# A conditioned residual block on one Trainium2 core: the convolution moved from full-array products on phase-split x to row-tiled, staggered products that read x at a step of 8 bytes

## What is computed

```python
# layer 0: grouped convolution (4 groups of 32 channels, 9 taps, padding 4), residual
out = conv1d(x, weight, padding=4, groups=4)
x   = x + out + (c @ c_weight.T)[:, :, None] + bias[None, :, None]
# layer 1: a 128x128 matrix per sample, mixed from 8 by attention on the condition, residual
att   = softmax(mlp(c))                        # 64 x 8
agg_w = einsum('bk,koi->boi', att, weight)     # one 128x128 matrix per sample
x     = x + einsum('boi,bih->boh', agg_w, x) + (att @ bias_k)[:, :, None]
```

## Time and profile before

| what | value |
|---|---|
| median of 3 runs | 840.06 us (839.46 to 840.33) |
| time of the profiled execution | 839.29 us |
| its span, first to last instruction | 837.4 us |
| TensorE busy (products) | 766.2 us, 92% |
| ScalarE, VectorE, GpSimd busy | 76%, 49%, 66% |
| mean granted TensorE clock | 0.977 of full |
| data moved by DMA | 242.90 MB, 290 GB/s |

### The profile page before, as it was taken

One profiled execution on the slowest core, in us unless ns is written; L12 is line 12 of the kernel. 1 busy time (PEld: TensorE's weight loads), 2 busy tenths in 40 slices (PEclk: granted clock), 3 DMA queues, 4 the chain that ended last, 5 costly groups with the idle time before them and its releaser, 6 DMA issues.

```text
span 837.4 us, 15303 instructions
## 1 busy us (share of the span) xinstructions
PE 766.2 (92%) x5424; PEld 600.9 (72%) x5424; DVE 410.1 (49%) x299; ACT 637.2 (76%) x291; POOL 552.1 (66%) x596
## 2 busy tenths in 40 slices
PE   2659998999999999999999999999999999999994
PEld 2547776777777777777777777777777777777773
DVE  6662455445445555444555445445554444554430
ACT  7766886888778877878786787888777868866554
POOL 3289686667778767767876666668667566866620
PEclk9988999999999999999999999999999999999997
DMA  5778999999999999999999999999999999987643
GB/s 194 206 230 263 309 317 292 305 326 306 325 314 330 313 313 308 318 301 306 329 318 306 297 312 312 319 331 332 305 314 300 284 305 327 319 257 247 220 164 126
DMA packets 91011, 242.90 MB, mean 290 GB/s; under 512 B 15914, under 2 KB 58482, under 8 KB 74610
## 3 DMA queue, kind: packets, MB, share of 16 engines
q1 hardware_dynamic: 90994, 242.67, 91.5%
HBM read 101.57 MB, written 75.50 MB: 211 GB/s over the span
## 4 chain that ended last, share of the span: by engine, by line
SPq 46%; PE 20%; DMA 20%; ACT 6%; issue 6%; POOL 1%; DVE 0%; POOLq 0%
SPq L240 34%; DMA mix_dram<-mix_parts 16%; PE ps L366 12%; SPq L264 9%; PE ps L383 8%; DMA mix_rep<-mix_dram 3%; ACT z_out L448 3%; SPq L272 2%; ACT x_ph L429 1%; ACT x_cv L452 1%; DMA x_in<-in_x_dram 1%; ACT z_out L452 0%; SPq L214 0%; PE ps L353 0%; POOL mix_prod L646 0%
## 5 line engine op out<-in xcount | busy, mean ns | idle before, releaser
L448 ACT ACTIVATE z_out<-ps,par 128x2048 f32<-128x2048 f32 x64 | 253.3, 3957 | 143.0 <-PE ps L383 143.0
L515 DVE TENSOR_TENSOR y_lo<-ps,y_hi 128x1024 fp32r<-128x1024 f32 x128 | 156.4, 1222 | 305.9 <-ACT y_hi L438 305.9
L429 ACT ACTIVATE x_ph<-x_in 128x2048 f32<-128x2048 f32 x63 | 246.5, 3914 | 0.0
L366 PE MATMUL ps<-x_hi,cw_hi 128*128 128x512 f32 x768 | 228.6, 406 | 0.3 <-DVE y_lo L515 0.3
L366 PE MATMUL ps<-x_hi,cw_lo 128*128 128x512 f32 x768 | 221.3, 397 | 0.0
L366 PE MATMUL ps<-x_lo,cw_hi 128*128 128x512 f32 x768 | 220.2, 395 | 0.0
L383 PE MATMUL ps<-y_hi,mix_rep 32*128 32x512 f32 x2048 | 179.7, 418 | 41.2 <-DMA mix_rep<-mix_dram 32.8
L366 PEld LDWEIGHTS ps<-x_hi,cw_hi 128*128 128x128 f32 x768 | 141.1, 191 | 52.2 <-issue 15.0
L366 PEld LDWEIGHTS ps<-x_hi,cw_lo 128*128 128x128 f32 x768 | 145.9, 190 | 33.9
L366 PEld LDWEIGHTS ps<-x_lo,cw_hi 128*128 128x128 f32 x768 | 145.4, 189 | 33.7
L438 ACT ACTIVATE y_hi<-ps 128x1024 fp32r<-128x1024 f32 x128 | 131.0, 1023 | 47.3 <-PE ps L366 47.3
(11 more groups left out here) (69 smaller groups left out, 87.8 us busy)
## 6 DMA issues: line engine op xcount, KB each, us to landing
x_in<-in_x_dram SPq DMA_DIRECT2D x64, 1024.0 KB, 6.2
out_dram<-z_out SPq DMA_DIRECT2D x64, 1024.0 KB, 5.9
x_cv<-x_ph SPq DMA_DIRECT2D x496, 128.0 KB, 3.8
mix_rep<-mix_dram SPq DMA_DIRECT2D x256, 128.0 KB, 4.0
mix_dram<-mix_parts SPq DMA_DIRECT2D x64, 128.0 KB, 2.7
mixw_nat<-in_L_cond_weight_dram SPq DMA_DIRECT2D x1, 512.0 KB
x_cv<-x_ph SPq DMA_DIRECT2D x8, 64.0 KB, 4.2
z_out<-in_L_cond_weight_dram SPq DMA_DIRECT2D x1, 144.0 KB, 2.2
```

Source lines behind the costliest of these rows:

```text
L366: mm = pe.matmul(y_ps[:, g, :], w[:, g, b, :], xx[buf(s)][:, g, b:b + N], start=n == 0, stop=n == len(terms) - 1)
L429: nc.scalar.activation(x_ph[pair_buf(s)][:, :, buf(s), :], x_in[buf(s)][:, :].rearrange("c (n q) -> c q n", q=PH), ACT.Copy).then_inc(x_sp ...
L448: nc.scalar.activation(z_out[buf(s)][:, :].rearrange("c (n q) -> c q n", q=PH), z_ps[:, :, :], ACT.Identity, bias=par[s[1]][:, NK:NK + 1]) ...
L515: nc.vector.tensor_tensor(y_lo[buf(s)][:, y_halves[h], :], y_ps[:, y_halves[h], :], y_hi[buf(s)][:, y_halves[h], :].bitcast(F32), ALU.subt ...
```

## The change

The phases and the moves are gone. x stays as it is loaded, 128 partitions = 4 groups x 32 channels. VectorE writes x_hi and x_lo in two planes h: plane h holds phases 2h and 2h+1 in turn, (h, column, e), so the reading side x_in is pairs of elements out of each four, and each plane is contiguous where it is written. ScalarE has no part in x any more.

A convolution product now has the 32 channels of one group as rows, and one position m of 12 (9 taps + 3, since four output phases share a read) as its shift; its 128 outputs are (output phase, output channel) as before. Its moving operand is one phase of x, 512 elements with a step of two elements. Each of the four groups works on its own 32-row tile of the array. A sample takes 12 x 3 x 4 = 144 such products, plus 48 for the mixing. Each tile runs through 36 steps of convolution and 12 of mixing, and tile t is four steps (`LAG`) behind tile t-1; the instructions of a step stand in the order tile 0, 1, 2, 3.

y is rounded and its rest made group by group, four pieces each, and z is taken in two pieces. x is loaded 3 samples ahead, not 7, and a load waits for x_lo of the sample that had its buffer. The setup network is put between the steps of the first convolution, taps have buffers of their own, and cw_hi and cw_lo hold the 12 positions: the nine taps' block copied four times, each shifted by one position and one output phase. The loop now covers 14 turns of four slots.

The diff, cut to its core:

```diff
-AHEAD = 7
+AHEAD = 3
+LAG = 4
...
+    M = K + PH - 1
+    CONV, MIX = 3 * M, 3 * G
+    STEPS = CONV + MIX
...
-        x_ph = two(sb, "x_ph", [P, PH, 2, N])
-        x_cv = two(sb, "x_cv", [P, G, 2, N])
-        x_hi = two(sb, "x_hi", [P, G, N + 2], F32R)
-        x_lo = two(sb, "x_lo", [P, G, N + 2], F32R)
+        x_hi = two(sb, "x_hi", [P, 2, N + 2, 2], F32R)
+        x_lo = two(sb, "x_lo", [P, 2, N + 2, 2], F32R)
+
+        def x_inner(tile):
+            return tile[:, :, 1:N + 1, :]
...
+        def x_at(tile, rows, m):
+
+            return tile[rows, m % PH // 2, m // PH:m // PH + N, m % 2]
...
-        cw_hi = sb("cw_hi", [P, G, 3, P], F32R)
+        cw_hi = sb("cw_hi", [P, M, P], F32R)
...
         def pipeline(eng, slot):
 
-            last = ROUNDS - (AHEAD + U - 1) // U
+            last = ROUNDS - 1
...
         def _(sp):
...
-                at_least(sp, x_split_ph, split)
+                at_least(sp, x_lo_made, taken)
                 sp.dma_start(x_in[buf(s)][:, :], x[b, :, :]).then_inc(x_loaded[buf(s)], DMA)
-
-            def move_x(s, phases, first=0, groups=range(G)):
...
             def slot(s):
+                load(after(s, AHEAD))
+                store_mix(s)
                 store(after(s, -2))
-                if not is_sample(s, 0):
-                    if s[1] % 2:
-                        move_x(after(s, 3), (0, 2))
-                    else:
-                        move_x(after(s, 2), (1, 3))
-                store_mix(s)
-                load(after(s, AHEAD))
                 load_mix(s)
...
         def _(pe):
...
+            between = {4: (turn_cond,), 10: (first_layer, turn_mixw), 20: (second_layer,), 28: (third_layer,),
+                       32: (context_mixed,), 44: (attention,)}
+
+            def conv_step(s, g, i):
...
+                rows = slice(Q * g, Q * g + Q)
+                if i == 0:
+                    if g == 0:
+                        pe.wait_ge(x_lo_made, done(s))
+
+                    at_least(pe, y_lo_made, done(s, G, lag=-2) + g + 1)
+                m, term = i // 3, i % 3
+                w, xx = ((cw_hi, x_hi), (cw_lo, x_hi), (cw_hi, x_lo))[term]
+                mm = pe.matmul(y_ps[:, g, :], w[rows, m, :], x_at(xx[buf(s)], rows, m),
+                               start=i == 0, stop=i == CONV - 1)
+                if i == CONV - 1:
                     mm.then_inc(y_ready, 1)
...
+            def mix_step(s, r, i):
...
+                rows = slice(Q * r, Q * r + Q)
+                if i == 0:
+                    if r == 0:
+                        pe.wait_ge(y_lo_made, done(s, G))
+                        pe.wait_ge(mix_loaded[buf(s)], DMA * G * (uses(s) + 1))
+
+                    at_least(pe, z_read, done(s, 2, lag=-2) + r // 2 + 1)
+                g, term = i // 3, i % 3
+                h, yy = ((0, y_hi), (1, y_hi), (0, y_lo))[term]
+                mm = pe.matmul(z_ps[:, r, :], mix_rep[buf(s)][rows, g, h, :], yy[buf(s)][rows, g, :],
+                               start=i == 0, stop=i == MIX - 1)
...
             def slot(s):
-                conv(s)
-                mix(after(s, -1))
...
+                for i in range(STEPS):
+                    if is_sample(s, 0) and i in between:
+                        for part in between[i]:
+                            part()
+                    for t in range(PH):
+                        if i >= LAG * t:
+                            step(s, t, i - LAG * t)
+                        else:
+                            step(after(s, -1), t, i - LAG * t + STEPS)
...
         def _(act):
-            def split_phases(s):
...
+                nc.scalar.activation(y_hi[buf(s)][:, g, :], y_ps[:, g, :], ACT.Copy).then_inc(y_hi_made, 1)
...
+            for r in range(PH):
+                copy(cw_hi[:, r:r + K, Q * r:Q * r + Q], wt_hi[:, :, :].bitcast(F32)).then_inc(cw_hi_placed, 1)
...
             def slot(s):
-                take_z(after(s, -2))
-                round_y(s, 0)
...
+                take_z(after(s, -2), 0)
+                take_z(after(s, -2), 1)
+
+                for g in range(G):
+                    round_y(s, g)
...
         def _(dve):
...
+            def round_x(s):
...
+                dve.wait_ge(x_loaded[buf(s)], DMA * (uses(s) + 1))
 
                 at_least(dve, y_ready, done(s, G, lag=-2))
-                nc.vector.tensor_copy(x_hi[buf(s)][:, :, 1:N + 1], x_cv[pair_buf(s)][:, :, buf(s), :]).then_inc(x_hi_made, 1)
+                nc.vector.tensor_copy(x_inner(x_hi[buf(s)]), x_in[buf(s)][:, :].rearrange("p (n h e) -> p h n e", h=2, e=2)).then_inc(x_hi_made, 1)
...
+                nc.vector.tensor_tensor(x_inner(x_lo[buf(s)]), x_in[buf(s)][:, :].rearrange("p (n h e) -> p h n e", h=2, e=2),
+                                        x_inner(x_hi[buf(s)]).bitcast(F32), ALU.subtract).then_inc(x_lo_made, 1)
...
             def slot(s):
...
+                if not is_sample(s, 0):
+                    round_x(after(s, 1))
+                    rest_x(after(s, 1))
+                for g in range(G):
+                    rest_y(s, g)
```

More of the change, by code:

```diff
@@ L219, in load @@
                     return
-                b, split = ahead(number(s), done(s, lag=-2))
-                at_least(sp, x_split_ph, split)
+                b, taken = ahead(number(s), done(s, lag=-2))
+                at_least(sp, x_lo_made, taken)
                 sp.dma_start(x_in[buf(s)][:, :], x[b, :, :]).then_inc(x_loaded[buf(s)], DMA)
-            def move_x(s, phases, first=0, groups=range(G)):
[L227 to L241, removed]
             def store_mix(s):
@@ L258, in load_mix @@
                 b = buf(s)
-                stored, mixed = ahead(DMA * (uses(s) + 1), done(s, lag=-2))
+                stored, mixed = ahead(DMA * (uses(s) + 1), done(s, PH, lag=-2))
                 sp.wait_ge(mix_stored[b], stored)
@@ L269, in store @@
                     return
-                b, read = ahead(number(s), done(s))
+                b, read = ahead(number(s), done(s, 2))
                 sp.wait_ge(z_read, read)
@@ L368, in conv @@
                     mm.then_inc(y_ready, 1)
-                    if is_sample(s, 0) and g == 2:
-                        attention()
-            def mix(s):
+            def mix_step(s, r, i):
                 if not exists(s):
                     return
-                pe.wait_ge(y_lo_made, done(s, 2))
-                pe.wait_ge(mix_loaded[buf(s)], DMA * G * (uses(s) + 1))
-                at_least(pe, z_read, done(s, lag=-1))
-                terms = [(g, h, yy) for g in range(G) for h, yy in ((0, y_hi), (1, y_hi), (0, y_lo))]
-                for n, (g, h, yy) in enumerate(terms):
-                    for r in range(PH):
-                        rows = slice(Q * r, Q * r + Q)
-                        mm = pe.matmul(z_ps[:, r, :], mix_rep[buf(s)][rows, g, h, :], yy[buf(s)][rows, g, :],
-                                       start=n == 0, stop=n == len(terms) - 1)
-                mm.then_inc(z_ready, 1)
@@ L412, in move_x0 @@
-        def move_x0(eng, groups, copy, moved):
-            eng.wait_ge(x_loaded[0], DMA)
             for g in groups:
-                for p in range(PH):
-                    n = copy(x_cv[0][Q * p:Q * p + Q, g, 0, :],
-                             x_in[0][Q * g:Q * g + Q, :].rearrange("c (n q) -> c q n", q=PH)[:, p, :])
-            n.then_inc(moved, 1)
+                rows = slice(Q * g, Q * g + Q)
+                write(wt_f[rows, :, :], wt_ps[rows, 0:K, Q * g:Q * g + Q]).then_inc(wt_copied, 1)
@@ L441, in take_z @@
[L441 to L448 removed]
+                act.wait_ge(z_ready, done(s, PH, lag=-1) + 2 * h + 2)
+                if h == 0:
+                    act.wait_ge(par_made, done(s))
+                    at_least(act, z_stored[buf(s)], DMA * uses(s))
```

327 lines of the change are left out of this document (131 added, 196 removed).

## The result

The changed kernel takes 1272.37 us (median of 4 runs, 1271.04 to 1272.63) against 839.76 us of the kernel before: ratio 1.516, interval 1.512 to 1.521. It is 52% slower. The time is inside the range, the sign is that of the forecast, and the size is not the forecast's 1464 us but close to that of its second rival, 1282 us.

The account below looks back on a forecast made before the run. TensorE, 92% busy and waiting for late mix_rep behind SyncE's moves, was taken as the bound. Start 15, waits 6, rounds 1428, last mixing 5.6 and end 8 gave 1462.5 us span, 1464 us in all; range 1240 to 1520.

Parts of the forecast that it names:

- Rival 2: TensorE's row tiles: a tile in the mixing can run ahead, 19.45 us a sample, 1282 us in all; chance 0.18.
- The price of the step: Convolution's moving read at a step of 8 bytes: 463 ns a round, by one 16-byte piece per 1.81 ns.
- The two-hit rule: Convolution's moving read: two hits per 16-byte line give full bandwidth, so the step is free, 232 ns a round.
- Rival 1: Convolution's moving read: the step is free, 232 ns a round, 762 us in all; chance 0.19.
- How rounds add up: TensorE's one queue: early tiles wait behind slow ones, so each of 48 rounds costs 463 ns, mixing included.
- What was held to be hidden: ScalarE 6.5, VectorE 6.5, GpSimd 8.6 us a sample, under TensorE's 11.1, and no wait on mix_rep: costed at nothing.
- Start and end: First convolution near 15 us, 6 us of waits; after the rounds 5.6 us last mixing, 8 us last z and store.
- Rival 3: TensorE's larger loop body fetched anew in each of 14 turns: at most 56 us; inside the range, no separate chance.

Follow-up runs that it names:

- e2_pairs: The changed kernel, but each convolution product reads 256 pairs of neighbouring values, a pair each 16 bytes (wrong columns): 1276 us.
- e1_contiguous: The changed kernel, but each convolution product reads 512 contiguous values in place of a step of 8 bytes (wrong columns): 767.04 us.
- e5_planes: The changed kernel with x_hi and x_lo split by VectorE into four planes, one a phase, so TensorE reads contiguous: 818.9 us, ratio to before 0.971.
- e10_shared: The four-plane version of the changed kernel, with two x_hi planes rounded by ScalarE and x_lo in two halves: 777.41 us, ratio to before 0.927.

## Why the prediction was right or wrong

- **The price of the step** (463 ns) was right in size: 452 measured, at either clock, as was said. That was luck, for the rule behind it turned out wrong in general. The two rows that agreed on 1.8 ns per 16 bytes agree by coincidence as far as TensorE goes: its contiguous read is 213 ns and an amount on top, and its stepped read is twice 213 and an amount on top. Had the change used a step of 16 bytes, the same argument would have forecast about 927 ns against 460.
- **The two-hit rule** of the Trainium skill ("SBUF — State Buffer", "Door 1: The DMA port swizzle"), by which the step would be free: the measurement decides against it for TensorE in float32r. Two accesses per piece run at half rate (e2_pairs, the changed kernel), four at the full one. Rival 1, 762 us, would have been right without the step: e1_contiguous gave 767.
- **How rounds add up** is the step that failed. "The instructions come from one queue in the order tile 0, 1, 2, 3, so a tile that is done early waits for its turn behind a slow one" put 463 ns on all 48 rounds. Measured, a product that waits for its tile doesn't hold back the other tiles at this interleaving, and each tile pays for its own 36 x 0.452 + 12 x 0.232 us. With the forecast's own prices that is 22.22 - 19.45 = 2.77 us a sample, 177 us for 64. Another 25 us are the price, 463 against 452 on 36 products. Together 202 us too much, and 10 us too little for start and end leave the miss of 192.
- **Rival 2** had the mechanism: its 19.45 us a sample stand against 19.06. That its 1282 us came so close is partly luck. With 452 ns it would have said 1257, and start and end took 52 us where it had 37. The range held the result only because it was drawn to take in this rival.
- **What was held to be hidden** was hidden: ScalarE is busy 34% and GpSimd 31%, and the waits of the changed kernel have none of TensorE on mix_rep. GpSimd takes 6.2 us a sample and not 8.6: its four small operations on 128x128 took 791 to 1352 ns before and take 460 now. As in e5_planes, VectorE's work on x is what can hold them off, and it now falls into GpSimd's idle time.
- **Start and end.** First convolution at 16.1 us (15 foreseen). From there to the last product at 1262.5 are 1246 us, 26 more than 64 samples; 17 were foreseen. Most of the surplus lies in sample 0, with its full-size products between the steps and 1.8 us idle between 42 and 60 us.
- **The code of the loop** costs nothing that shows: queue 8 moved 0.29 MB in the whole run, against 0.18 and 14 turns of 98 KB, and TensorE is busy for all of the 1120 us from 80 to 1200, with no gap at a turn. Rival 3 falls.
- **A slip in rival 1:** by its own sum, with 13.6 us for the end and 3000 rounds, a round at which both kernels are equal is (837 - 50 - 13.6)/3000 = 258 ns, not 255. Nothing hangs on it.

## What to carry to other kernels

Before a layout makes TensorE read its float32r moving operand at a step, count the accesses that fall in each 16 bytes: with two or one the product took twice the time at the upper clock, whether the step was 8, 16 or 32 bytes, so half-measures such as pairs bring nothing. Put the strided access on an engine that has slack, as in e10_shared, and look in the timeline at what runs beside it. Products on different row tiles may be priced tile by tile if their instructions are finely interleaved in the queue. If many of one tile stand in a row, price them nearly one after the other: blocks of 12 took 60.1 us a sample, of 4 20.33.

## What the hardware showed that was not expected

A product whose columns are all one value takes 216 ns where contiguous ones take 231, so 15 ns of a contiguous float32r product hang on what it reads. At a granted clock near half, contiguous products take 427 ns and stepped ones 450, so the step is nearly free there, and at the upper clock it doubles the time. A step of 32 bytes (431 ns) is cheaper than one of 16 (460) or of 8 (452). TensorE starts products of a free row tile ahead of waiting ones of another, but in blocks of 12 the next tile starts only when three of the block are left: 19.06, 20.33 and 60.1 us a sample for blocks of 1, 4 and 12. GpSimd's work stands still while VectorE reads x_in for x_lo: 1038 ns when they don't meet, and 5.60 us for two products where they do.
